# Constant products on TensorE in the waits between the last attention group and the experts of a perceiver layer

## What is computed

```python
x = x + xattn(layernorm(x), ctx)     # 32 batches of 32 tokens of 512; 257 keys of 384; 16 heads of 64
x = x + attn(layernorm(x), ...)      # 16 heads of 32; q, k and v are one projection
x = x + ffn(layernorm(x), ...)       # 8 experts, the 2 best of each token

def ffn(x):
    logits = (x @ gate_w + gate_b) / 0.9
    keep = top 2 of 8;  p = softmax(where(keep, logits, -inf))
    h = gelu(x @ w1[e] + b1[e]);  o = h @ w2[e] + b2[e]       # 512 -> 2048 -> 512
    return layernorm(sum_e p[e] * o[e]) * ln_g + ln_b
```

## Time and profile before

| | us |
|---|---|
| median of 3 runs (lowest, highest) | 1473.92 (1472.44, 1474.47) |
| the profiled execution, its own time | 1473.72 |
| its span, first to last instruction | 1472.1 |
| TensorE busy | 1371.9 (93%) |
| VectorE, ScalarE, GpSimd busy | 780.4, 586.5, 152.4 |
| mean granted TensorE clock | 0.972 |
| share of the chain that ended last: TensorE, VectorE, ScalarE | 82%, 7%, 4% |

### The profile page before, as it was taken

One profiled execution on the slowest core, in us unless ns is written; L12 is line 12 of the kernel. 1 busy time (PEld: TensorE's weight loads), 2 busy tenths in 40 slices (PEclk: granted clock), 3 DMA queues, 4 the chain that ended last, 5 costly groups with the idle time before them and its releaser, 6 DMA issues.

```text
span 1472.1 us, 24339 instructions
## 1 busy us (share of the span) xinstructions
PE 1371.9 (93%) x7888; PEld 870.2 (59%) x7889; DVE 780.4 (53%) x1871; ACT 586.5 (40%) x1082; POOL 152.4 (10%) x200
## 2 busy tenths in 40 slices
PE   6879999999999999999985699999999999999997
PEld 5658677686776876768764344444444444444442
DVE  5665876878778777777665442222222222232225
ACT  3565665756757567465670211212112121121100
POOL 1001012020120200202003100000000000000005
PEclk9999999999999999999996799999999999999997
DMA  9693142341323413224028807523325166100005
GB/s 364 265 351 144 52 156 91 115 160 50 141 95 112 173 50 126 110 97 190 29 114 328 307 17 278 206 93 148 144 104 195 35 265 248 44 21 21 14 15 171
DMA packets 53566, 207.48 MB, mean 141 GB/s; under 512 B 4902, under 2 KB 5012, under 8 KB 47388
## 3 DMA queue, kind: packets, MB, share of 16 engines
q1 hardware_dynamic: 40320, 123.14, 22.8%
q0 software_dynamic: 13184, 83.89, 14.9%
q10 hardware_dynamic: 28, 0.01, 0.0%
HBM read 144.11 MB, written 62.91 MB: 141 GB/s over the span
## 4 chain that ended last, share of the span: by engine, by line
PE 82%; DVE 7%; ACT 4%; issue 4%; DMA 1%; POOL 1%; SPq 0%; DVEq 0%; ACTq 0%
PE bank L623 21%; PE bank L1458 8%; PE bank L1416 7%; PE bank L605 6%; PE bank L606 5%; PE bank L607 5%; PE bank L1379 4%; PE bank L1484 4%; PE bank L1400 3%; PE bank L615 3%; PE bank L1506 2%; PE bank L1425 2%; PE bank L1440 2%; ACT moe_w L951 2%; PE bank L1459 1%
## 5 line engine op out<-in xcount | busy, mean ns | idle before, releaser
L623 PE MATMUL bank<-moe_w,arena 128*128 x736 | 330.9, 592 | 0.0
L491 DVE SCALAR_TENSOR_TENSOR arena<-bank,now_scales,arena 128x512 f32<-128x512 f32 x92 | 69.1, 751 | 346.1 <-PE bank L607 346.1
L623 PEld LDWEIGHTS bank<-moe_w,arena 128*128 128x128 f32 x736 | 132.7, 190 | 132.5 <-issue 132.5
L1416 PE MATMUL bank<-moe_w 128*128 128x257 f32 x768 | 189.9, 385 | 6.5 <-DVE moe_w L883 6.5
L428 ACT ACTIVATE arena<-arena 128x512 f32<-128x512 f32 x92 | 58.3, 633 | 337.8 <-DVE arena L491 337.8
L1416 PEld LDWEIGHTS bank<-moe_w 128*128 128x128 f32 x768 | 138.2, 192 | 25.7 <-DVE moe_w L883 5.8
L605 PE MATMUL bank<-moe_w,arena 128*128 x368 | 140.6, 382 | 2.4 <-DVE arena L504 2.4
L606 PE MATMUL bank<-moe_w,arena 128*128 x368 | 140.4, 382 | 0.0
L607 PE MATMUL bank<-moe_w,arena 128*128 x368 | 140.2, 381 | 0.0
L1458 PE MATMUL bank<-moe_w 128*128 128x512 f16 x384 | 114.4, 379 | 10.0 <-ACT moe_w L940 7.0
L926 ACT ACTIVATE moe_w<-bank,cols,ugain 128x512 f32<-128x512 f32 x96 | 74.6, 777 | 61.6 <-PE bank L1459 60.8
(11 more groups left out here) (230 smaller groups left out, 2129.1 us busy)
## 6 DMA issues: line engine op xcount, KB each, us to landing
moe_w<-w_halves POOLq DMA_DIRECT2D x8, 4096.0 KB, 13.3
moe_w<-in_L_ffn_w_dram POOLq DMA_DIRECT2D x8, 4096.0 KB, 24.4
w_halves<-moe_w SPq DMA_DIRECT2D x48, 512.0 KB, 2.7
xs_rows<-blocks SPq DMA_DIRECT2D x8, 2048.0 KB, 14.8
moe_w<-in_L_ffn_w_dram SPq DMA_DIRECT2D x16, 1024.0 KB, 6.4
arena<-in_ctx_dram SPq DMA_DIRECT2D x32, 384.0 KB
arena<-in_L_ffn_w_dram SPq DMA_DIRECT2D x8, 1024.0 KB, 4.8
blocks<-in_L_ffn_w_dram SPq DMA_DIRECT2D x8, 1024.0 KB, 4.8
```

The costliest lines, as they stand in the source:

```text
L491: nc.vector.scalar_tensor_tensor(out=h_sb[:, fb % 2, :], in0=bank[fb % 2][:, :], scalar=now_scales[:, KD:KD + 1], in1=b1_rows[:, bass.ds(s ...
L623: last = nc.tensor.matmul(Y[:, :], hT_sb[:, fb % 2, c, :], moe_flat[:, bass.ds((e % 2) * 16384 + 8192 + (4 * fb + c) * DIM, DIM)], start=( ...
L1416: last = nc.tensor.matmul(bank[h][:, 0:KEYS], qkT[:, c, b, h * P:(h + 1) * P], cnT[:, b % 2, c, :], start=(c == 0), stop=(c == KC - 1))
```

## The change

`ident16` is the unit matrix's memory read as f16 (128 x 256; each f32 1.0 becomes 0 and 1.875, all else is 0). A product of its first 128 columns with all 256 goes into `bank[1]`, which nobody reads at that time. Such products are put into TensorE's program, 154 in all: 142 in the last `body` (g = 8), in six of its waits, and 12 between `xt_fill(0)` and the first `mm1`. They wait for nothing and signal nothing. The bodies of g = 0 to 7, the other 22 jobs and the other engines' programs are unchanged.

```diff
+        ident16 = ident[:, :].bitcast(F16)
@@ moe_pe @@
             xt_fill(0)
+            for _ in range(12):
+                nc.tensor.matmul(bank[1][:, 0:2 * P], ident16[:, 0:P], ident16[:, :], start=True, stop=True)
             job(0, True, False)
@@ TensorE's program @@
+            def keep_running(n):
+
+                for _ in range(n):
+                    nc.tensor.matmul(bank[1][:, 0:2 * P], ident16[:, 0:P], ident16[:, :], start=True, stop=True)
@@ body @@
                         qk_proj(g, i)
+                    if do_b and not do_a and i == 1:
+                        keep_running(16)
                     if do_b and i == 1:
                         y_fill(g - 1, YT_AT, 2 * (g - 1) + 1, y)
@@
                         if do_b and b == 1 and c == 1:
+                            if not do_a:
+                                keep_running(10)
                             ss_fill(g - 1)
                         if do_b and b == GB and c == 1:
+                            if not do_a:
+                                keep_running(40)
                             pv_fill(g - 1)
@@
+                if do_b and not do_a:
+                    keep_running(14)
                 if do_b:
                     y_fill(g - 1, YT2_AT, 2 * g, y2)
@@
                     wo_proj(g, 1)
+                if do_b and not do_a:
+                    keep_running(6)
                 if do_b:
                     rk_fill(g - 1)
+                if do_b and not do_a:
+                    keep_running(56)
```

## The result

| | before | after |
|---|---|---|
| median of 6 runs each, measured side by side (lowest, highest) | 1475.01 (1472.44, 1475.78) | 1468.70 (1466.85, 1470.81) |
| ratio, 95% interval | | 0.9959 [0.9946, 0.9972] |
| the profiled execution: its own time, span | 1473.72, 1472.1 | 1469.05, 1467.4 |
| mean granted clock | 0.972 | 0.985 |

The kernel is faster by 4 to 8 us in this comparison. The larger part of that difference is the kernel before, whose median was 1475.01 the first time and 1473.00 the second; that of the kernel after was 1468.70 and 1469.82. The forecast, 1470.3, which is 3.6 us less or a ratio of 0.9976, lies between the two.

What follows compares the result with a forecast made beforehand. The last body was taken as a chain with TensorE steps at low clock, the experts as TensorE-bound. Gains of 1.9 ahead of the scatter and 1.7 at `mm1` make 3.6 us: 1470.3, range 1467.8 to 1473.4.

Steps and rivals of the forecast that it cites:

- Fillers cost nothing: All 154 fillers: 0.108 us each at high clock, about 0.215 at low, covered by their waits, so costed at nothing.
- `y_fill` and `kq_fill` 0: Start of the last body: steps end up to 2.6 us sooner, but copies wait for POOL's zeroed tile; 0 us gained.
- `ss_fill` 0: Scores in the last body: could save 0.86 us, but the longer wait before it loses the clock; 0 us gained.
- `pv_fill` and `ws_fill` 1.48: Behind the 40 fillers: clock high at `pv_fill`, so 1.94 becomes 1.08 and 4.22 becomes 3.60 us.
- `lg_fill` and `rk_fill` 0.4: Routing steps of the last body: 1.4 us if the clock stays high; expected to fall more often than not, so 0.4.
- Sum ahead of the scatter 1.9, bound 1.9: Gains of the last body up to the scatter sum to 1.9 us; the scatter takes no more than about 1.9.
- Floor at 813.6: Last scatter, behind expert 0's loads on POOL's queue, lands not before 813.6, 1.9 us sooner than before.
- the rival without a floor: Scatter gets through beside the loads, or copies beat the memset: 5.9 us gained, 1468.0; chance 0.12.
- `xt_fill` and first `mm1` 1.7: Start of the experts: clock low at `xt_fill`; twelve fillers start dense work 3.4 us sooner, `mm1` gains 1.7 us.
- That only the last twelve count: Rival: clock falls again before each burst of the last body, leaving 1.7 us gained, 1472.2; chance 0.2.
- That fillers don't raise the clock: Rival: no burst gets shorter and three waits are outlasted, 3.7 us more, 1477.6; chance 0.05.
- That the fillers do nothing either way: Rival: the waits move with other things, so the time stays within 1 us, 1473.5; chance 0.08.

Runs made afterwards that it cites:

- after_again: The kernel after, unchanged, measured once more in the next batch: 1469.82 us, ratio 0.9981 to the kernel before.
- d_8rows: The kernel after with both operands of all 154 fillers cut to 8 rows, same columns: 1476.42 us, ratio 1.0027 to the kernel before.
- f_heads_first: The kernel after, but in the last group POOL zeroes `blocks` only after the four head copies: 1470.22 us, ratio 0.9983 to the kernel before.
- i_rows_later: The kernel after with SP's three row loads issued behind the second job's rows: 1467.61 us, ratio 0.9964 to the kernel before.
- b_body_only: The kernel after without the twelve fillers ahead of `mm1`, the other 142 kept: 1469.70 us, ratio 0.9987 to the kernel before.
- c_no56: The kernel after without the 56 fillers behind `rk_fill`: 1468.13 us, ratio 0.9972 to the kernel before.
- j_heads_rows: The kernel after with the edits of `f_heads_first` and `i_rows_later` together: 1465.81 us, ratio 0.9958 to the kernel before.
- l_full: `j_heads_rows` with filler counts raised to 27, 28, 62, 26, 14, 92, 22: 1470.96 us, ratio 0.9987 to the kernel before.
- m_full_plain: The kernel after with filler counts raised to 27, 40, 62, 26, 14, 92, 22: 1471.76 us, ratio 0.9995 to the kernel before.
- a_only12: The kernel after with only the twelve fillers ahead of `mm1`, the other six counts set to 0: 1469.60 us, ratio 0.9983 to the kernel before.

## Why the prediction came out as it did

**The total was right, and the terms less so.** 3.6 forecast; 3.81 in the stretch of the first profile and 2.16 in that of `after_again`; about 6 and 3 us by the two ratios. That the first profile comes within 0.2 is partly luck: 1.34 ahead of `xt_fill` instead of 1.9, and 2.47 behind it instead of 1.7. Point by point:

- *Fillers cost nothing: right.* No step of the kernel after started later for one, in either profile. At the high clock they were 0.109 us apart (92 of them took 10.20, 26 took 3.01), at the low one 0.216 (`d_8rows`), as estimated; a weight load that did not hide would have shown in these distances.
- *`y_fill` and `kq_fill` 0: right in size, wrong in a word.* 2.6 us of `kq_fill` shrank to 0.29 at `ss_fill`. POOL's zeroed tile was not finished "whatever TensorE does": it came at 779.85 instead of 780.43, and 0.37 of that is the whole stretch starting sooner, so 0.2 is left. Then two copies slipped in ahead of the memset, the third was stretched to 2.13 beside it, and all ended at 783.3. `f_heads_first` shows that the memset costs 1.7 us. In the kernel before too only one was stretched, the four taking 1.35, 0.42, 0.42 and 0.43, not 0.6 to 0.7 each. The Trainium skill, "SBUF — State Buffer", the section "SBUF: two separate sides", has the first of the two engines to start hold the shared port pair for its whole length. The trace agrees in that one engine waits for all of the other's instruction: one copy, the memset and three copies would be an estimated 0.42 + 1.80 + 3 x 0.42 = 3.48, and 3.43 was measured. It does not show the page's order: by the records the third copy started 0.04 us ahead of the memset (780.75, 780.79) and waited all the same.
- *`ss_fill` 0: right.* 1.94, low clock, the wait before it grown from 2.17 to 3.60.
- *`pv_fill` and `ws_fill` 1.48: the step that failed in size.* It said "the clock is high at `pv_fill`". From `pv_fill` to `y_fill` the gain was 0.12 (10.09 to 9.97), in `after_again` too. The clock was high, but too soon: it rose at 786.14, 2.7 us after `ss_fill` began instead of 5.5, so the 40 took 4.92 and not 7.0, and the 2.10 us left empty lost it at 792.97. Where the 40 ran longer at the low clock they lasted (6.2 to 6.6 us), and the term is there: 8.71 or 8.72 from `pv_fill` to `y_fill` in `i_rows_later`, `b_body_only` and `c_no56`, 1.37 us less than before, about the forecast. Where they were over in 4.54, in `f_heads_first` and `j_heads_rows`, it is 1.4 to the other side (11.50), and `l_full`, which is `j_heads_rows` with 62 in place of the 40 and the other counts raised too, has 8.72 again, and so has `m_full_plain`. So the term hangs on the empty end of the wait: with 2.0 to 2.5 us of it empty the clock was lost, with 0.8 or less it was not.
- *`lg_fill` and `rk_fill` 0.4: mis-sized to the other side.* From `y_fill` to the first scatter's issue 7.46 went to 6.49, 0.97. The clock was high from 796.38 to 806.62 and did not fall in the waits there. Over the eight profiles with all 142 of these fillers and `c_no56`, the forecast holds better: in six the clock fell by the end of `lg_fill`, as it had expected of most, and those gained 0.17 to 0.66; the other three gained 0.97 to 1.15. From `pv_fill` to the first scatter's issue, against 1.48 + 0.4 = 1.88 forecast, it was 1.09 and 1.27 in the two profiles of the kernel after, and 1.54, 1.70 and 2.03 in `b_body_only`, `i_rows_later` and `c_no56`; the three with the copies first lost 0.95.
- *Sum ahead of the scatter 1.9, bound 1.9: 1.34 measured at `xt_fill`.* To the first scatter's issue it was 1.38 = 0.29 + 0.12 + 0.97: short by 1.36 at `pv_fill`, over by 0.29 and 0.57 at the other two.
- *Floor at 813.6: right to within 0.7 us, and firmer than the first profile shows.* The last scatter landed at 813.89, which is 41.73 us after `y_fill` where the forecast comes to 41.07. In the kernel after the floor took little: counted from `y_fill` the first scatter was issued 1.38 us sooner than before, and the last landed 1.21 sooner. `l_full` and `m_full_plain` confirm it: 2.0 and 3.8 us of earlier routing turned into a scatter of 8 us. So the rival without a floor is out. What it is made of was half right: SP's row loads, named in the forecast, are 0.6 to 1 us of it (`i_rows_later`); moving the bias load did not shorten it.
- *`xt_fill` and first `mm1` 1.7: 2.47 in the profile after, 0.96 in `after_again`, 1.45 in `a_only12`.* Right on average: the nine profiles with twelve full fillers there have a mean of 1.81. The expected clock at `xt_fill` is wrong for the first: it stood high over 2.87 us of idling. The Trainium skill, "TensorE: Matmul & The Clock Gate", Part 1, calls the number of slow products at a start run-variable; the traces agree: `mm1` ran low for 0, 1.6 and 2.6 us in executions with the same twelve ahead of it.

**The rivals.** That only the last twelve count was given 0.2. `a_only12` and `b_body_only` measure 0.9983 and 0.9987, so each part has its share, yet `a_only12`'s interval holds `after_again`'s ratio, so the other 142 are shown to add something only by their own run. That fillers don't raise the clock is false for 128 rows and true for 8. One row against it proves less than it was taken for: the transposes from 22.0 to 24.0 follow without a gap on dense products that began at 11.56, at a clock that was already high, so they show nothing of what raises it. That the fillers do nothing either way (0.08) is out: both intervals of the kernel after end below 1.

**Its own signs.** The copies ended at 783.3 (forecast about 784), the scatter landed at 813.89 (813.5 to 814), and `mm1` came 3.20 after `xt_fill` (3.4). The clock was high from 785 to 803 but for 1.1 and 3.4 us, and just there it should have shortened `pv_fill` and `ws_fill`, which took 1.40 and 4.65 (1.1 and 3.6).

**Left open.** Why expert 0's load goes out 1.65 us later with more fillers; and what the best counts would be. Up to `rk_fill` the raised ones kept the clock and ended in time (`ss_fill` and `pv_fill` at 9.59 and 17.64 in `l_full`, 9.59 and 17.63 in `j_heads_rows`); in the two waits behind it none did both. The raised counts of the body with the old 56 and 12 were not run.

## What to carry to other kernels

Fillers in waits are worth at most the low-clock excess of the steps behind them, less what the next floor takes: find the floor first (here a scatter behind 9 MB of loads on its own queue), because past it a gain upstream comes back as a longer DMA (8.35 us in `l_full`). Fill a wait to its end at the high clock only where the clock comes in high, as in the body of `l_full`; where it may come in low, count the run at the low clock, as the 22 ahead of `mm1` show, which held it up by 1.1 and 2.1 us. Put the run that matters directly ahead of the dense work: twelve products ahead of `mm1` gave as much as 142 others. Use all 128 rows.

## What the runs showed of the hardware that was not expected

- **The clock stayed low beside products of 8 rows and was high beside products of 128 rows that are nearly all zeros.** Those of 8 rows kept TensorE 95% busy for 23.89 us at 0.50 (`d_8rows`). Those of 128 rows, whose operands are zero but for at most one element in each row, ran among the body's steps through 47.42 us at 1.00 (`m_full_plain`), and in the kernel after the clock rose beside them, at 786.14.
- **The clock dips elsewhere, and not in every execution.** In the profiles before and after, two early stretches were below full clock, where `d_8rows`, whose program is the same there, had none. The columns are those of the stretches above. First the kernel before:

```profile
34.00:40.00 6.00, 5.47 (x64) 5.28 (x64) 3.14 (x5) 1.76 (x3) 0.00 (x0) 0.72 1.07 385
54.00:62.00 8.00, 5.85 (x25) 4.22 (x26) 6.41 (x14) 3.85 (x12) 0.21 (x1) 0.79 0.03 13
```

  And the first of the two in `d_8rows`:

```profile
34.00:40.00 6.00, 4.27 (x65) 4.04 (x66) 4.59 (x9) 2.76 (x5) 0.00 (x0) 1.00 1.07 387
```

  The last body began at 772.5 and 772.2 in the first two and at 769.2 to 771.4 in the ten executions profiled without these dips; the two others that had them began it at 772.0 and 773.1. This is a part of the 5 to 6 us between runs of one kernel (before: 1469.87 to 1476.09 in 29 runs), and more than most terms of the sum. The other end varies too: from the first `hT_fill` to the end of the span it is 639.5 to 642.7 us in the fourteen profiles.
- **A small load moved can be a load moved in front of something else.** The bias load taken from ahead of the scatter made the rows' load 3.98 and 4.42 instead of 2.69.
